# Score groups of three and three banks instead of four and two, with sums and feed-forward pieces placed to match

## What is computed

```python
x_norm = _layernorm(x, gamma, beta)
q, k = l2_normalize(heads(x_norm @ w_q)), l2_normalize(heads(x_norm @ w_k)); v = heads(x @ w_v)
align = jnp.einsum('bhqd,bhkd->bhqk', q, k)
resonance = 0.5 + 0.5 * jnp.tanh((align - COLLAPSE_THRESHOLD) * SHARPNESS)
modulation = resonance * gate_q[..., :, None] * gate_k[..., None, :]
fused = jnp.einsum('bhqk,bhkd->bhqd', modulation, v)        # then @ w_o + b_o
x = _layernorm(x + attention);  x = _layernorm(x + ffn(x))
# ffn: fp4_linear(silu(fp4_linear(x, w_gate)) * fp4_linear(x, w_up), w_down), inner width 704
```

## Time and profile before

| | |
|---|---|
| time, median of 2 runs | 4471.53 us (4471.3 to 4471.76) |
| the profiled execution | 4469.53 us, span 4467.7 us |
| PE busy | 4139.1 us (93%) |
| ACT busy | 4026.8 us (90%) |
| DVE busy | 1558.9 us (35%) |
| POOL busy | 159.2 us (4%) |
| mean granted clock of TensorE | 0.985 |
| chain that ended last | PE 68%, ACT 16%, issue 8%, DVE 4%, DMA 2%, SP's queue 2% |
| its largest lines | PE 1213 34%, PE 1203 19%, ACT 660 15%, PE 1240 7%, PE 1263 4% |
| loop over units | 346.8 to 4382 us |

### The profile page before, as it was taken

The page is one execution under the profiler, slowest core; times in us unless marked ns, Lnnn a source line. Parts: engine busy times, 40 slices in busy tenths (PEclk is TensorE's granted clock), DMA queues, the critical chain, the costliest instruction groups (busy, mean ns, idle before and its releaser), DMA issues.

```text
span 4467.7 us, 80907 instructions
## 1 busy us (share of the span) xinstructions
PE 4139.1 (93%) x28776; PEld 1293.7 (29%) x28776; DVE 1558.9 (35%) x4536; ACT 4026.8 (90%) x3275; POOL 159.2 (4%) x120
## 2 busy tenths in 40 slices
PE   7977889999999999999999999999999999999997
PEld 5651222222222222222222222222222222222223
DVE  6772013233333323332333332333233333333235
ACT  4658999999999999999999999999999999999993
POOL 2330000000000000000000000000000000000001
PEclk9989999999999999999999999999999999999998
DMA  3445433443344434443344334433444344434440
GB/s 110 125 116 83 61 61 61 76 76 60 57 75 77 64 61 67 77 67 62 63 77 70 61 62 77 77 60 61 72 77 64 63 66 76 72 57 64 77 80 14
DMA packets 180059, 315.51 MB, mean 71 GB/s; under 512 B 65265, under 2 KB 141809, under 8 KB 154609
## 3 DMA queue, kind: packets, MB, share of 16 engines
q1 hardware_dynamic: 179568, 309.41, 41.2%
HBM read 266.82 MB, written 42.47 MB: 69 GB/s over the span
## 4 chain that ended last, share of the span: by engine, by line
PE 68%; ACT 16%; issue 8%; DVE 4%; DMA 2%; SPq 2%; POOL 0%; ACTq 0%; POOLq 0%; DVEq 0%
PE ps L1213 34%; PE ps L1203 19%; ACT room L660 15%; PE ps L1240 7%; PE ps L1263 4%; DMA m_f<-fused_t 1%; DVE room L807 1%; SPq L486 1%; PE ps L1158 0%; SPq L462 0%; DVE st L761 0%; DMA vt<-v_gated 0%; DVE xnT L797 0%; PE ps L1225 0%; PE ps L1169 0%
## 5 line engine op out<-in xcount | busy, mean ns | idle before, releaser
L660 ACT ACTIVATE room<-ps 128x1024 f32<-128x1024 f32 (+1 forms) x2816 | 3792.9, 1416 | 246.2 <-PE ps L1203 231.7
L1213 PE MATMUL ps<-room,vt 128*32 128x512 f32 x16384 | 2064.4, 605 | 0.0
L1203 PE MATMUL ps<-qs,room 64*128 64x512 f16 x8198 | 1330.5, 384 | 249.5 <-ACT room L660 214.3
L1203 PEld LDWEIGHTS ps<-qs,room 64*128 64x128 f16 x8198 | 311.2, 93 | 1802.3 <-ACT room L660 1133.9
L1213 PEld LDWEIGHTS ps<-room,vt 128*32 128x32 f32 x16384 | 389.7, 109 | 954.8 <-issue 954.8
L1240 PE MATMUL ps<-wguT,m_xqT 128*128 128x352 f32 x960 | 348.2, 485 | 0.0
L905 DVE TENSOR_TENSOR vz<-ps,vz 128x352 f32<-128x352 f32 x120 | 63.0, 525 | 757.7 <-ACT vz L665 757.7
L910 DVE TENSOR_TENSOR vz<-ps,vz 128x352 f32<-128x352 f32 x120 | 63.0, 525 | 595.9 <-PE ps L1240 595.9
L1263 PE MATMUL ps<-wdnT,wqk 128*128 128x256 f32 x720 | 198.9, 404 | 0.6 <-DVE wqk L875 0.6
L1240 PEld LDWEIGHTS ps<-wguT,m_xqT 128*128 128x128 f32 x960 | 162.6, 189 | 105.2 <-issue 54.3
L561 POOL TENSOR_TENSOR m_x<-m_x,bo 128x256 f32<-128x256 f32 x60 | 43.6, 727 | 3972.7 <-DMA m_x<-in_L_attn_x_dram 3972.7
(11 more groups left out here) (165 smaller groups left out, 2211.0 us busy)
## 6 DMA issues: line engine op xcount, KB each, us to landing
room<-k_parts SPq DMA_DIRECT2D x520, 256.0 KB, 9.8
vt<-v_gated SPq DMA_DIRECT2D x65, 1024.0 KB, 17.5
qs<-q_parts SPq DMA_DIRECT2D x520, 32.0 KB, 10.4
gqb<-q_gates SPq DMA_DIRECT2D x256, 64.0 KB, 2.1
room<-in_L_attn_x_dram SPq DMA_DIRECT2D x16, 512.0 KB, 4.2
v_gated<-vz SPq DMA_DIRECT2D x64, 128.0 KB, 2.1
q_parts<-room SPq DMA_DIRECT2D x32, 256.0 KB, 2.1
k_parts<-room SPq DMA_DIRECT2D x32, 256.0 KB, 2.2
```

The lines of the kernel that those rows point to most:

```text
L660: act.activation(res[:, c, o:o + m, :], ps[:, o:o + m, :], ACT.Sigmoid, scale=2 * SHARP / QK_UP ** 2, bias=-2 * SHARP * THRESH).then_inc(b ...
L1203: ins = pe.matmul(ps[:, BANK[n % 2] + i, :], ks[o:o + HROWS, par, h // 2, kt * P:(kt + 1) * P], qs[o:o + HROWS, par, h // 2, :], start=Tru ...
L1213: ins = pe.matmul(ps[32 * h:32 * h + 32, SUM_BANK, :], vt[:, par, n * HD:n * HD + 32], r, start=kt == 0, stop=kt == KT - 1, skip_group_che ...
```

## The change

The 4 and 2 banks of the first forty groups become 3 and 3, and odd groups begin at bank 3. Sums: one key tile at step 4c, two at step 4c + 2, where it was two and one. The pieces P, X, G0 to G3, D0 and D1 and the two gate sigmoids move two steps ahead; H0 and H1 stay. The number of reads, scores, sums and pieces is the same.

```diff
-GROUPS = [4, 2] * 20 + [2, 2, 2, 2]
-BANK = (0, 4)
+GROUPS = [3, 3] * 20 + [2, 2, 2, 2]
+BANK = (0, 3)
...
         if c:
-            at[4 * c] = [3 * c - 1, 3 * c]
-        at[4 * c + 2] = [0, 1] if c == 0 else [3 * c + 1]
+            at[4 * c] = [3 * c - 1]
+        at[4 * c + 2] = [3 * c, 3 * c + 1]
...
-BEGIN = {7: "P", 19: "X", 23: "G0", 27: "G1", 31: "G2", 35: "G3"}
-END = {0: "H0", 3: "H1", 11: "D0", 15: "D1"}
-GATE_ACT = {25: 0, 29: 1}
+BEGIN = {5: "P", 17: "X", 21: "G0", 25: "G1", 29: "G2", 33: "G3"}
+END = {0: "H0", 3: "H1", 9: "D0", 13: "D1"}
+GATE_ACT = {23: 0, 27: 1}
```

## The result

The changed kernel takes 4881.07 us, median of 2 runs (4877.33 to 4884.8), against 4471.53: 1.0917 of the time before, with a 95% interval of 1.0897 to 1.0937. It is 9.2% slower. The prediction was 4842 us, with 4750 to 4930 as its range.

A forecast was written before the change was run, and what follows sets the result against it. PE was taken as the bound wherever there is a piece, with ACT waiting for it. Longer periods (274 + 8 us) and P's wait (89 us) made 371 us on 4469.5, so 4842 us as median; range 4750 to 4930.

The forecast's parts named there:

- A lone score: On PE, the third score of a group costs a pair's time: 0.54 us to the next full-array work, not 0.32.
- The loop: Through PE and ACT, release to release over a four-group period: 5.07 us plus the piece, 6.45 with G, 6.56 with D.
- A period without a long piece: Four groups with no long piece on PE: ACT stalls 0.51 us, making 5.87 us against 5.67.
- The lower bound: PE's own work alone in a period with G: 6.14 us, 112 us a run less, left out of the range.
- 4.56 us a unit: Added time in each of the sixty units with pieces, from longer periods on PE and ACT: 274 us in all.
- 274 + 8: Longer periods: 274 us over the sixty units with pieces, 8 us over the first four without.
- P's wait: PE before line 1225: P, moved ahead of m_f, waits 2.2 us in 45 units, 99 us less 10 already paid: 89.
- rival (2): PE's granted clock falls to half after P's waits, costing 45 to 90 us: 4887 to 4932 us; chance 0.12.
- (1): At line 1225 P's wait for m_f stays hidden, by earlier SP issue or more ACT reads left: 4754 us; chance 0.10.
- (3): On PE a lone score costs nothing of its own; only P's wait remains: about 4560 us; chance 0.05.
- (4): Equal halves cover the double sum on PE evenly, so ACT's nine stalls a unit go: 236 us, 4235 us; chance 0.03.

The follow-up runs named there:

- m_f first: The changed kernel with SP issuing the four loads of gates behind the load of m_f instead of before it, P still at step 5: 4734.3 us, 1.06.
- the first experiment: The changed kernel with only P put back from step 5 to step 7: 4769.71 us, 1.066 of the time before.
- the wait filled: The changed kernel with seven more matmuls, their result unused, on PE just before P's wait for m_f: 4821.4 us, 1.0799.

## Why the prediction was right, and where it was off

**The scores and the loop: right.** A lone score was given the time of a pair, 0.54 us; it takes 0.53 to 0.54. The loop was 6.45 us with G and 6.56 with D; measured 6.45 with G, 6.56 with D0 and 6.65 with D1. A period without a long piece was 5.87; measured 5.87. The experiment without the lone score removed 0.63 of the 6.45, and the one with parted sums exchanged the loop for PE's total. The lower bound I had for a G period, 6.14, is within 0.02 us of what PE's own work takes there (6.45 less its wait of 0.33), and it did not bind.

**4.56 us a unit: right.** Sixty units with P in time take 4051.1 us (m_f first), 259 more than before; the first four 8.6 more in that trace, 8.0 in the changed kernel's. That is 267 us where the sum had 274 + 8 = 282. But counted over periods of four groups that hold no stretch at 0.50, a unit takes 67.4 us with m_f first and 62.9 before, 4.5 more, which is 271 us in sixty units. The other 12 us are stretches at 0.50: nine made the kernel before slower, which was in its time but not in the periods that I compared, and only four are left with m_f first.

**P's wait: right in mechanism, mis-sized.** The term was 99 us of waits less 10 already paid. PE waited 100.5 us. P was ready 6.7 us after fs, as said. That the two sums of waits are so near is luck in part: the units at the start of an iteration were left out as covered by the pause, and they waited 10.7 us, while the other 45 waited 2.0 us each and not 2.2. And the wait cost more than its own length: with P in time the sixty units are 142 us shorter, where the term had 89. Of these 53 us, 17 are P's later start (106 us in the table above) and 36 go with the clock.

**The step that was mis-sized is the one that gave the clock nothing in the forecast and kept it apart as rival (2).** It was not one or the other. Of the 30 waits of 1.6 us and more (up to 4.4) 18 were followed by a stretch at 0.50, or ended in one, and of the 30 units with a shorter wait none. I set one wait of 1.08 us without a fall against the rival; but the waits that I forecast were of about 2 us, as long as the pause of 2.00 us in the earlier trace rows, behind which the clock had fallen. The forecast missed by 39 us, and that is a sum in which errors cancel: 53 too low for P and the clock, 15 too high through the time before. Against the kernel before the falls cost less than the 36 us: it was at half clock for 47.8 us of its loop and the changed kernel for 102.4, and half of the difference, 27 us, is the most that they can have added. Rival (2) had 45 to 90. The Trainium skill (TensorE: Matmul & The Clock Gate, Part 1) says that the throttled state is the default and that activity releases it. A clock at 0.50 behind a wait of 2.62 us fits that; but of the 22 waits between 1.60 and 2.61 us 10 had a fall and 12 had none, so the length of a wait does not decide it alone.

**The rivals.** (1) P's wait hidden: fell, by the first experiment and by SP's order. (3) the lone score for nothing: fell, 345 us. (4) faster: fell; the double step still stalls ACT, by 0.40 us where it was 0.30 in the earlier trace rows:

```profile
2513.40 1.45 ACT L660 ACTIVATE room<-ps 128x1536 f32<-128x1536 f32 x1 [0.40 <-PE ps L1203]
```

Not foreseen was that the pieces had no need to move.

Left open: why SP issues m_f 6.1 us behind fs in the last unit of each iteration of the changed kernel, and 5.2 us in the same units with the wait filled, where SP's queue is the same. Open too is why m_f landed 2.75 us after its issue in the mean of the changed kernel's first profile and 2.42 in its second: the issue stood at the same place in both (6.04 and 6.01 us behind fs), so it is the landing that made the waits 100.5 and 85.5 us. And no run tells which of the longer waits a fall will follow.

## What to carry over

When two engines pass buffers back and forth, write down the loop through both: release, write, other work in the writer's queue, write, hand over, read. Compare it with each engine's total; here the longest of them was the period (the loop's 6.45 us, and PE's 6.51 once the sums were parted). Even halves help only if the writer's cost is even too: here scores come in pairs, and a group of three pays for four. And before a consumer is moved ahead, measure how long its input has been there, down to the issue queue that brings it.

## What the hardware showed that I had not expected

A wait of PE costs more than its length if the clock falls behind it. In the changed kernel 18 waits of 1.6 to 4.4 us were followed by 3.4 to 6.8 us at half clock, and 12 between 1.6 and 2.6 us were not, so it can be priced only in the mean. In the kernel before, 8 of the 9 stretches stand at the pause of 1.7 to 2.2 us with which an iteration starts. And two groups of three scores back to back take 0.82 us, as six in groups of four and two do, while each of them alone takes 0.60: the halves of the array pair across the boundary of a group when nothing stands between.
